# Norming the next item in front of copying the present transposes, and aggregating in front of a pair's sums, in a six-stage float32 block

## The reference

```python
x = x + 0.5 * quant_ffn(layernorm(x))      # x @ w.T + bias, w dequantised from 6-bit codes
x = x + s4_conv_0(layernorm(x))            # causal convolution along the 512 columns, as a Toeplitz product
x = x + 0.5 * quant_ffn(layernorm(x))
x = x + 0.5 * swiglu(layernorm(x))         # silu(x Wg^T) * (x Wu^T) Wd^T, width 1376
x = x + s4_conv_1(layernorm(x))
x = x + 0.5 * swiglu(layernorm(x))
```

## Time and profile before

| | us |
|---|---|
| runs, median of 3 | 929.58 (926.26 to 929.59) |
| profiled execution, its own time | 929.4 |
| its span in the trace | 927.6 |
| items 0 to 55, until PE starts the first unit | about 195.6 |

### The profile page before, as it was taken

One profiled execution on the slowest core, in us unless ns is written; L12 is line 12 of the kernel. 1 busy time (PEld: TensorE's weight loads), 2 busy tenths in 40 slices (PEclk: granted clock), 3 DMA queues, 4 the chain that ended last, 5 costly groups with the idle time before them and its releaser, 6 DMA issues.

```text
span 927.6 us, 11675 instructions
## 1 busy us (share of the span) xinstructions
PE 880.4 (95%) x4088; PEld 723.7 (78%) x4088; DVE 621.4 (67%) x1054; ACT 315.2 (34%) x518; POOL 372.0 (40%) x729
## 2 busy tenths in 40 slices
PE   3989999689999999999999999999999999999998
PEld 2777887567777788788888887888888778888877
DVE  6778786687898879665556686555566875444452
ACT  4523454643334435222224361222233622222121
POOL 5975356852323235323324353332333542222211
PEclk9989999999999999999999999999999999999999
DMA  9300000027666786554655565555465757666345
GB/s 313 137 0 1 1 1 1 1 113 250 228 217 237 271 295 191 171 182 134 195 153 155 171 189 177 178 149 181 130 189 157 221 145 238 204 204 204 125 139 179
DMA packets 41594, 149.05 MB, mean 161 GB/s; under 512 B 3520, under 2 KB 3776, under 8 KB 40128
## 3 DMA queue, kind: packets, MB, share of 16 engines
q0 software_dynamic: 29040, 100.93, 36.3%
q1 hardware_dynamic: 12496, 47.37, 14.0%
HBM read 118.14 MB, written 30.15 MB: 160 GB/s over the span
## 4 chain that ended last, share of the span: by engine, by line
PE 74%; DVE 14%; POOL 5%; issue 3%; DMA 2%; ACT 2%; SPq 0%; DVEq 0%; ACTq 0%; POOLq 0%
PE front L1369 14%; PE front L1371 13%; PE front L1370 13%; PE acc L1323 6%; PE acc L1325 6%; PE acc L1324 6%; PE front L446 3%; PE acc L1260 3%; PE acc L1259 3%; PE acc L1258 3%; DVE hidden_lo L1189 3%; DVE weight_operands L575 2%; DVE snapshots L1149 2%; POOL x_rows L718 2%; DVE gate_up L1149 1%
## 5 line engine op out<-in xcount | busy, mean ns | idle before, releaser
L1369 PE MATMUL front<-row_operands_hi,weight_operands 128*128 128x512 f32 x616 | 243.4, 395 | 9.0 <-DVE snapshots L1149 8.1
L1371 PE MATMUL front<-row_operands_hi,weight_operands 128*128 128x512 f32 x616 | 240.8, 391 | 0.0
L1370 PE MATMUL front<-row_operands_lo,weight_operands 128*128 128x512 f32 x616 | 240.4, 390 | 0.0
L1369 PEld LDWEIGHTS front<-row_operands_hi,weight_operands 128*128 128x128 f32 x616 | 116.1, 188 | 37.7 <-issue 10.3
L1323 PE MATMUL acc<-down_weights,hidden_hi 128*128 128x512 f32 x352 | 140.1, 398 | 3.6 <-DMA down_weights<-saved_down 1.7
L1149 DVE TENSOR_TENSOR snapshots<-front,snapshots 128x512 f32<-128x512 f32 x132 | 91.0, 689 | 78.3 <-PE front L1371 77.0
L1325 PE MATMUL acc<-down_weights,hidden_lo 128*128 128x512 f32 x352 | 137.3, 390 | 0.0
L1324 PE MATMUL acc<-down_weights,hidden_hi 128*128 128x512 f32 x352 | 137.2, 390 | 0.0
L1371 PEld LDWEIGHTS front<-row_operands_hi,weight_operands 128*128 128x128 f32 x616 | 115.9, 188 | 24.8
L1370 PEld LDWEIGHTS front<-row_operands_lo,weight_operands 128*128 128x128 f32 x616 | 116.2, 189 | 23.4
L788 POOL DMA_DIRECT2D weight_operands<-saved_weights x66 | 48.6, 737 | 185.5 <-PE front L1371 180.6
(11 more groups left out here) (159 smaller groups left out, 1353.9 us busy)
## 6 DMA issues: line engine op xcount, KB each, us to landing
weight_operands<-saved_weights POOLq DMA_DIRECT2D x33, 1280.0 KB, 6.4
down_weights<-saved_down POOLq DMA_DIRECT2D x77, 512.0 KB, 4.1
saved_weights<-weight_operands SPq DMA_DIRECT2D x11, 1792.0 KB, 8.2
weight_operands<-saved_weights POOLq DMA_DIRECT2D x33, 512.0 KB, 4.5
raw_weights<-wgu SPq DMA_DIRECT2D x11, 512.0 KB, 4.5
saved_down<-down_weights SPq DMA_DIRECT2D x11, 512.0 KB, 3.3
x_rows<-x_in SPq DMA_DIRECT2D x3, 1024.0 KB, 13.6
out<-x_rows SPq DMA_DIRECT2D x3, 1024.0 KB, 5.0
```

The lines of the kernel that those rows point to most:

```text
L1369: T.matmul(o, wh, xh, start=(j == 0), stop=False)
L1370: T.matmul(o, wh, xl, start=False, stop=False)
L1371: last = T.matmul(o, wl, xh, start=False, stop=(j == 1))
```

## The change

In the loop over the items ScalarE now issues the norm of n+5 ahead of the copy of n+4 (or the pair's copies), where it was behind. VectorE, in an iteration whose n+4 is a prep item, issues the aggregate of n+7 ahead of the pair's work.

```diff
             for n in range(PRE):
+
                 m = n + XT_AHEAD
+                if n + NORM_AHEAD < PRE:
+                    norm_step(act, n + NORM_AHEAD)
                 if m < PRE and is_light(m):
                     xt_hi_step(act, m)
                 elif m < PRE and second_of_pair(m):
                     pair_copies(act, ITEMS[m].number // 2)
-                if n + NORM_AHEAD < PRE:
-                    norm_step(act, n + NORM_AHEAD)
                 if n + 3 < PRE and second_of_pair(n + 3):
                     sums_hi_step(act, ITEMS[n + 3].number // 2)
...
                 if is_light(n):
                     update_step(dve, n)
                 m = n + XT_AHEAD
+                works_on_pair = m < PRE and not is_light(m)
+                if n + STATS_AHEAD < PRE and works_on_pair:
+                    aggregate_step(dve, n + STATS_AHEAD)
                 if m < PRE and is_light(m):
                     xt_lo_step(dve, m)
                 elif m < PRE and second_of_pair(m):
                     pair_sums(dve, ITEMS[m].number // 2)
                     pair_lows(dve, ITEMS[m].number // 2)
-                if n + STATS_AHEAD < PRE:
+                if n + STATS_AHEAD < PRE and not works_on_pair:
                     aggregate_step(dve, n + STATS_AHEAD)
```

## The result

The changed kernel takes 931.33 us (median of 18 runs, 929.04 to 933.43), the one before beside it 928.05 (18 runs, 925.37 to 930.02). The ratio is 1.004, with a 95% interval of 1.0032 to 1.0048: slower by 3.3 us at the medians, certain in its sign and under the 0.5% that the prediction takes as telling. The forecast was 933.5 against a before of 929.58, so +3.9. Measured it is +3.3 by the medians, and the ratio put on 929.58 would be 3.7. The 931.33 itself lies in the whole range of 928.5 to 937 but under the 932.5 to 935 that the first case had for itself, since the before beside it is 1.5 us lower than the one that the forecast was added to.

The account below looks back on a forecast made before the run. Between the products no engine is full, so waits between engines set the pace. Longer laps less gains give +2.5, with half clock +4.0: 929.4 + 4.0 = 933.4 profiled, 933.5 as median; own range 932.5 to 935, whole range 928.5 to 937.

Parts of the forecast that it names:

- first case: Main forecast, delay plus half clock before unit 0: 933.5 us, own range 932.5 to 935, chance 0.50.
- The loop: Pairs' copies queue behind a norm awaiting POOL's rstd, itself behind L524: laps 11.50, then 11.77 with the aggregate, against 10.72.
- (b): At the first pair on ACT, the rounded sums L518 come one norm sooner: 0.70 us gained.
- (a): Item 44's norm runs ahead of the copy, so PE's 1.54 us wait at 158.54 ends 0.6 us earlier, partly won.
- (c): PE's 0.50 us wait for a norm at 119.07 in the convolution mostly goes: 0.4 us gained.
- VectorE's part: Aggregate ahead of a pair's sums: 0 alone; with ScalarE's part takes one rstd (1.2 us) out of each lap.
- The place where the delay reaches the end: Through POOL's bias, DVE's update and first sum of unit 0, PE restarts 2.5 us late, at 203.4 instead of 200.86.
- The half clock: PE idles 3.1 us before 193.54, then runs slow, losing 1.6 us; the restart is some 4.0 us late.
- No half clock: Rival: no half clock in front of unit 0, so +2.5 only, 931.9 to 932.1 us; chance 0.24.
- The waits are removed: Rival: PE's waits for norms simply go, 6 x 1.54 + 0.4 = 9.6 us less, 919.9; chance 0.04.
- copies pass a waiting norm: Rival: ACT lets copies pass a waiting norm; 1.1 us less, 928.3; within the 0.10 for 926.5 to 929.
- The bound by POOL alone: POOL's own work sets laps of 10.1 us: 2.9 us less, 926.5; within the 0.10 for 926.5 to 929.

Follow-up runs that it names:

- fourth experiment: The changed kernel plus ten matmuls on PE in front of its waits for the low parts of pairs 1 to 3; 931.24 us, ratio 1.0042.
- third: The changed kernel, but at the four iterations with a pair's copies these stand in front of the norm again; 926.31 us, ratio 0.998.
- fifth experiment: The changed kernel with ScalarE's norm first only at the four iterations with a pair's copies, light items' copies first as before; 933.54 us, ratio 1.0063.
- first experiment: The changed kernel with VectorE's order put back as before, so ScalarE's swap alone; 933.11 us, ratio 1.0062.
- sixth: The changed kernel with POOL's second L524 of each pair one iteration later, behind the next rstd; 928.1 us, ratio 0.9995.
- second experiment: The changed kernel with ScalarE's order put back as before, so VectorE's earlier aggregate alone; 928.53 us, ratio 1.0008.
- eighth: The changed kernel with copies first at pairs, norm first elsewhere, and POOL's second L524 one iteration later; 925.45 us, ratio 0.9969.
- seventh experiment: The kernel before with ScalarE's swap in iterations 0 to 31 only, VectorE as before; 927.45 us, ratio 0.9992.

## Why the prediction was right

**The loop is what it said.** Its signs are in the trace: laps of 11.74, 11.77 and 11.76 (forecast 11.50, 11.77, 11.77; the two terms of the later laps, 11.50 and 0.25, add up to 11.75); L484 directly behind a norm that waited for POOL, 2.78 us at 164.84 and 2.50 at 188.39; PE waits of 3.23 and 3.21 us on L513; half clock near 193. Pair 2 fits less well, with a norm's wait of 0.89 us where 2 to 3 were forecast and a PE wait of 2.67. With PE kept busy (fourth experiment) that norm waits 2.50 us, so the 0.89 comes from the half clock at pair 1. The third and fifth experiments show that the four pair iterations alone make the loop. Its length follows its steps: with one rstd more in it the laps are 1.11 and 0.79 us longer (first experiment), with one L524 less 1.39 to 1.41 shorter (sixth).

**Its first lap was mis-sized, 11.50 for 11.74.** The aggregate's 0.25 us is not in this lap. The norm at 164.84 began 0.56 us after the start of the rstd's last instruction (164.28), where the sum has 0.29 for this. The same 0.56 to 0.57 us stands there in the first, fourth, fifth and sixth experiments, so it isn't chance; its cause stays open.

**The gains ahead of the pairs: right, and a little small.** (b) is exact: from the first copy L484 of pair 0 (153.16) to L524 it takes 4.88 us, before 5.58. The rest of the 1.38 us by which the first L524 is early, 0.68, is what (a), (c) and the convolution's own variation give, for which the sum had 0.4. How little a single trace settles this is seen in the fourth experiment: its program is the same up to there, and its L524 came 0.65 later. In the medians (c) can't be seen.

**VectorE's part: right.** Alone 0 (second experiment); with ScalarE's part it is worth 1.6 us over three laps (first experiment). The prediction named one rstd, 1.2 us, in each lap; measured it is 1.11, 0.79 and -0.29, so the sign is right and the size under half.

**The place where the delay reaches the end: right, with 0.3 missing.** From the first L524 to the restart at 209.21 there were 49.79 us, now 54.58, so +4.79. Of this the laps are +3.82 (35.27 against 31.45; forecast 3.6), the half clock 0.65 by the fourth experiment, and 0.3 remain. That experiment shows it: POOL's last first-half L524 takes 1.73 us, in the earlier trace rows 1.43, and the bias and DVE's update come later by it. With the 1.38 won in front, +3.41 at the restart; the forecast was 4.0.

**The half clock: foreseen, its price wrong.** This is the term that was clearly mis-sized. The stretch came where it was expected, behind the wait of 3.21 us, and PE lost what was forecast: records of 0.63 us, from 193.77 on some eight of them 0.43 instead of 0.23 apart. But the prediction let all of it but 0.25 us through to the restart ("It just fits"), since by its sum PE was done 0.25 us ahead of DVE's first sum. By the fourth experiment, where the clock stays up, it is 0.63: L524's extra 0.3 us delays DVE's sum and not PE. So some 0.9 of 1.5 us could pass; 0.79 is seen at the product behind that sum (204.41 against 204.27, each from its own first L524), and 0.65 at the restart; the medians are too coarse for it. In the change DVE is late by it too: its update at 197.84 waited 1.12 us for PE, and the same update in the fourth experiment doesn't wait. The price of a delay on one chain is what is left when the slack against the other is taken off, and that slack is only as well known as the worse of the two chains. The Trainium skill's rule for this ("TensorE: Matmul & The Clock Gate", Part 1), by which the throttled state is the default and activity releases it, agrees with the fourth experiment, where ten matmuls in the gap kept the full clock. What the prediction read out of it, that the longest wait costs most, holds only in part: five waits of 3.21 to 3.23 us were followed by half clock (two in the change, three in the first experiment), but one of 3.22 in the fifth was not, and the 2.67 of the change was not. So it was partly luck that the stretch came where the sum had it. The sums it put beside each other, 4.0 with the half clock and 2.5 without, came out as 3.4 and 2.8 in the traces.

**The rivals.** "No half clock" was +2.5, as near to the measured +3.3 as the forecast's 4.0, and for the wrong reason: there was a stretch, and its weight was small. "The waits are removed" and "copies pass a waiting norm" are out by the laps; ScalarE's L484 at 165.56 stood behind its waiting norm while its data were there (its transposes ran at 161.72), as the strict FIFO of the Trainium skill says (same page, "Architectural detail: the array is 16× 32×32, not 1× 128×128"). The bound by POOL alone, which that rival put at 10.1 us a lap, is real once the loop is open: 10.02 to 10.05 in the third and eighth experiments, with 926.31 and 925.45 us where it had 926.5; that is 1.3 and 2.5 us under before, for its 2.9. Of the 4 us that the prediction let the ready norm stand behind the copy at 157.10, ACT was idle for 1.13; in the rest it had other work in front.

**What this amounts to.** At the medians the change cost 3.3 us; the forecast was 3.9. In the traces it is 3.4 for 4.0: 0.85 less for the clock, 0.2 more for the laps, 0.3 more for the last pair's L524, and 0.3 less through what was won in front.

## What to carry to other kernels

An instruction that is issued early costs its engine nothing only if what it waits for doesn't depend on what stands behind it: before moving one ahead in an in-order queue, follow its releaser back, and where the chain comes round to the moved-past instruction, add up the lap. The list of waits names the target but not this; PE's matmuls waited for the norm 7 times, and at the pairs it waited itself for POOL. If the early place is wanted anyway, take it where the input is long ready (here the light items), and shorten the loop on the engine that has the movable step.

## What the runs showed of the hardware

A wait of PE of one and the same length is followed by half clock in some executions and not in others. The wait at the restart is 2.18 to 2.20 us in every kernel here; in seven of the ten profiled executions half clock follows (the granted clock from 205 to 225 us is 0.91), in three (the first, second and seventh experiment) none does (1.00). At the pairs five waits of 3.21 to 3.23 us were followed by it and a sixth, of 3.22 in the fifth experiment, was not; nor were the sixth experiment's of 2.65, 2.36 and 2.38 us. PE in the second experiment's profiled execution, whose span is 924.0 us, and then in the eighth's, 924.1:

```profile
207.29 0.47 PE L1373 MATMUL front<-row_operands_hi,weight_operands 128*128 128x512 f32 x1 [2.18 <-DVE snapshots L1153]
```

```profile
205.71 0.47 PE L1376 MATMUL front<-row_operands_hi,weight_operands 128*128 128x512 f32 x1 [2.19 <-DVE snapshots L1156]
...
207.60 0.63 PE L1377 MATMUL front<-row_operands_lo,weight_operands 128*128 128x512 f32 x1
```

No record of 0.63 us follows the first, and from 225 us on the granted clock is 1.00 in all ten executions. From that row to the end of the span it takes 716.7 us in the second experiment, 716.2 in the first and 716.8 in the seventh; in the seven with the half clock it takes 718.1 to 718.9 (718.4 in before, 718.9 in the change). So one such stretch costs 1.3 to 2.7 us there, and the one at the last pair 0.65, where other engines were late too. Two profiled executions can differ by some 2 us for this alone: the second experiment's span is 3.6 us under that of before, while its median is 0.9 above.

It also makes part of the spread between the runs of one kernel. Of the 51 runs of before beside the experiments, the 19 with a granted clock of 0.993 or less have a mean of 929.0 us, the 19 with 0.996 or more one of 927.0. What in an execution decides it, these traces don't tell.
